# The second cross-attention of a perceiver kernel: from transposed exponentials to transposed scores

## The chip, the cores and the metric

The kernel runs on one core of one Trainium2 chip. The metric is the device time of one execution in microseconds (us): the median over several executions. Engines are named as in the profile: PE is TensorE (matrix products), PEld its weight loads, DVE VectorE, ACT ScalarE, POOL GpSimd, SP SyncE, whose queue issues the transfers (DMA). SBUF is the on-chip memory with 128 partitions, PSUM the memory of eight banks into which PE writes (a bank holds 512 fp32 values in each partition), HBM the memory of the chip. fp32r is a form of fp32 operands for PE; this kernel splits a value into a high part, rounded to that form, and a low part, the rest, and adds three products (high by high, high by low, low by high) where it wants fp32 accuracy.

## The reference

Two layers work on x of 16 batches by 64 rows by 256 features. Each reads a context `ctx_1024` of 16 x 1601 x 256. The first layer is a cross-attention with top-32, a retention step and an attention block with a mixture of experts. The second layer is the cross-attention in question, then random features, then three tree-shaped feed-forward parts. What the changed stage computes is this, with 16 heads of width 16:

```python
def _L1_xattn_ref(q, k, v, ...):            # q: layernorm(x); k = v = ctx_1024
    b, l, _ = q.shape
    ...
    qn = layernorm(q, norm_w, norm_b)
    kn = layernorm(k, norm_w, norm_b)
    vn = layernorm(v, norm_w, norm_b)
    Q = (qn @ Wq + bq).reshape(b, l, H, E)
    K = (kn @ Wk + bk).reshape(b, s, H, E)
    V = (vn @ Wv + bv).reshape(b, s, H, E)
    scale = 1.0 / jnp.sqrt(jnp.asarray(E, Q.dtype))
    scores = jnp.einsum('blhe,bshe->bhls', Q, K)
    A = jax.nn.softmax(scale * scores, axis=-1)
    O = jnp.einsum('bhls,bshd->blhd', A, V)
    O = O + Q
    out = jnp.transpose(O, (0, 2, 1, 3)).reshape(b, l, H * E)
    return layernorm(out, norm1_w, norm1_b) @ Wo + bo + out
```

Per batch there are 1601 context rows, kept as 13 chunks of 128 (the last has 65), and 16 heads x 64 queries, which makes 1024 softmax rows of 1601 scores.

## The kernel before

The program is a chain of stages. The one that changes is `phase_heads_read`, which begins with loading its parameters, normalises x and projects the queries, then goes through 16 batches, two to a turn of a loop, and ends by mixing heads and projecting the output.

**A batch.** SP loads the 1601 rows of 256 features, a context row on a partition (L1277). POOL normalises them with mean and reciprocal deviation that an earlier stage left (L1313, 13 instructions). PE transposes them into features by rows (L1386, 26 products); ACT and DVE split these into high and low (`rowsT`, L1634). Two projections follow, in units that the code calls fills: the keys, transposed, in 8 quarters of 400 to 402 columns with 6 products each (L1392), and the values, a chunk of 128 rows by 256 in 6 products (L1399), 7 fills of two chunks. ACT writes the high keys (L1518), DVE the low ones, in halves of 64 partitions (L1646), and ACT the values (L1524).

**Scores and softmax.** The 16 heads go in 8 pairs. For a pair, PE makes four quarters of scores, 128 queries (2 heads x 64) by 402 keys, two products each (L1415): the queries stand alone in their own 16 rows of a block of 128 otherwise zero, which POOL writes (`pairq`, L1328), and high and low keys stand in the two halves of the partitions. DVE takes the maximum of all 1608 columns in one instruction over four banks (L1609), ACT makes the exponentials in four instructions (L1535) into `exps` with a running sum, PE transposes `exps` chunk by chunk (L1436, 13 a pair, 104 a batch), and DVE and ACT copy the result from PSUM to `probT` (L1619, L1625, L1543). After four pairs PE weighs the values (L1454: 13 chunks x 4 products, each on a column tile of 32), and the result is divided by the sums, which are transposed for that (L1433).

**What sets the order.** The order on each engine is written out by hand: `PE_STEPS`, `ACT_STEPS` and `DVE_STEPS` give for each of the 8 pairs a string of steps (S scores of the next pair, W weigh, 0 to 3 the four groups of transposes, a to d fills of the next batch, M maximum, H and I heads and inverses), and `SLOT_FILLS` says which fills stand in which pair. The fills use banks 6 and 7 in turn, the scores banks 0 to 3, the transposes 4 and 5. After the last batch DVE adds the value bias and the queries for all rows (L1738).

## Time and profile before

| what | value |
|---|---|
| time, median of 3 executions | 1908.88 us (1906.41 to 1911.81) |
| the profiled execution: span from first to last instruction | 1909.7 us |
| PE busy over the span | 1562.7 us, 82% |
| DVE, ACT, POOL busy | 1234.9, 866.1, 370.7 us |
| `phase_heads_read`, from its first to its last instruction | 522.4 to 1641.7 us |
| of it start, 16 batches, end | 80.8, 995.6, 42.9 us |

Of the profiled execution the profile gives the span; its own time stands nowhere apart from it, and the span lies inside the three times listed. The 1909.7 us are one execution and the sums below are made against them. A busy PE says little by itself, since matrix products overlap in the pipeline and the profile models their ends: the cost of a group of products is read from the start of its first to the start of what follows on PE. An "idle before" is the gap ahead of a group and the engine's work, or the transfer, that ended it.

### The profile page before, as it was taken

To read this page: it belongs to the slowest core of one execution; us is meant where nothing else is said; L and a number is where in the kernel's file an instruction comes from. 1 tells how busy PE (TensorE), PEld (TensorE's weight loads), DVE (VectorE), ACT (ScalarE), POOL (GpSimd) and SP (SyncE) were. 2 spreads that over 40 slices of the span, in tenths; PEclk is the share of its full clock that TensorE was granted. 3 is DMA by queue.
4 is the path that set the end of the run, shared out by engine and by line. 5 is a ranking of instruction groups with operands and counts; after the bars stand their busy time and mean duration, and the time that the engine had idled before them with its cause. 6 is when DMAs were issued, how large, how long until landed. Compare 5 with 4: busy or idle time off the path is not lost. (4 is left out here: it accounts for less than half of the span.)

```text
span 1909.7 us, 32902 instructions
## 1 busy us (share of the span) xinstructions
PE 1562.7 (82%) x11828; PEld 1276.4 (67%) x11828; DVE 1234.9 (65%) x2268; ACT 866.1 (45%) x2127; POOL 370.7 (19%) x444
## 2 busy tenths in 40 slices
PE   7888876679557988988889888888898885649997
PEld 4555554469546877877778778777787773436665
DVE  4999745743554777777777767777678674554443
ACT  2444411220014666656666657566666662123322
POOL 0000000010031344224322432243224000031110
PEclk9777788679858999999999999999999997779999
DMA  9577206005030111011101110111010001020000
GB/s 331 207 278 283 90 1 254 1 1 177 10 123 1 37 37 37 1 38 37 37 2 37 37 38 1 38 37 37 2 37 1 1 1 45 14 118 38 1 1 22
DMA packets 74561, 118.97 MB, mean 62 GB/s; under 512 B 1312, under 2 KB 66976, under 8 KB 73376
## 3 DMA queue, kind: packets, MB, share of 16 engines
q1 hardware_dynamic: 74400, 116.76, 17.4%
q8 instruction: 109, 1.79, 0.4%
q14 instruction: 52, 0.43, 0.1%
HBM read 114.66 MB, written 2.10 MB: 61 GB/s over the span
## 5 line engine op out<-in xcount | busy, mean ns | idle before, releaser
L1535 ACT ACTIVATE d_exps<-psum,d_negmax 128x400 f32<-128x400 f32 (+1 forms) x512 | 297.8, 595 | 37.8 <-DVE d_negmax L1609 35.3
L1436 PE MATMUL psum<-pk,d_exps 128*128 128x128 f32 (+1 forms) x1664 | 265.8, 277 | 20.9 <-DVE d_probT L1619 11.7
L1415 PE MATMUL psum<-d_keys,d_pairq 128*128 128x402 f32 x1024 | 248.8, 376 | 20.6 <-issue 13.2
L1609 DVE TENSOR_REDUCE d_negmax<-psum 128x1 f32<-128x1608 f32 x128 | 234.4, 1831 | 48.4 <-PE psum L1415 46.9
L1646 DVE SCALAR_TENSOR_TENSOR d_keys<-psum,d_bk,d_keys 64x400 fp32r<-64x400 f32 (+1 forms) x256 | 162.4, 634 | 115.5 <-ACT d_keys L1518 108.7
L1313 POOL TENSOR_SCALAR d_rowsN<-d_rowsN,d_rowmoments 128x256 f32<-128x256 f32 x195 | 235.8, 1224 | 0.1
L1436 PEld LDWEIGHTS psum<-pk,d_exps 128*128 128x128 f32 (+1 forms) x1664 | 200.0, 141 | 47.9 <-DVE d_probT L1619 19.8
L1415 PEld LDWEIGHTS psum<-d_keys,d_pairq 128*128 128x128 f32 x1024 | 179.7, 195 | 55.6 <-ACT d_exps L1535 36.4
L1392 PE MATMUL psum<-d_rowsT,d_wk 128*128 128x400 f32 (+1 forms) x768 | 173.8, 362 | 19.6 <-DVE d_keys L1646 18.8
L1619 DVE COPY d_probT<-psum 128x512 f32<-128x512 f32 x256 | 174.0, 687 | 23.7 <-PE psum L1436 19.2
L1543 ACT ACTIVATE d_probT<-psum 128x512 f32<-128x512 f32 x128 | 76.6, 599 | 234.3 <-PE psum L1436 232.8
L1399 PE MATMUL psum<-d_wv,d_rowsT 128*128 128x256 f32 (+1 forms) x1248 | 178.0, 292 | 0.0
L1518 ACT ACTIVATE d_keys<-psum,d_bk 64x400 fp32r<-64x400 f32 (+1 forms) x256 | 151.5, 592 | 57.9 <-PE psum L1392 56.3
L1399 PEld LDWEIGHTS psum<-d_wv,d_rowsT 128*128 128x128 f32 (+1 forms) x1248 | 157.7, 189 | 0.0
L1392 PEld LDWEIGHTS psum<-d_rowsT,d_wk 128*128 128x128 f32 x768 | 133.9, 192 | 27.4 <-issue 25.9
L1386 PE MATMUL psum<-pk,d_rowsN 128*128 128x128 f32 (+1 forms) x416 | 71.3, 287 | 79.6 <-DVE d_rowsT L1634 20.3
L1323 POOL TENSOR_TENSOR d_fence<-row_mean 128x1 f32<-128x1 f32 x32 | 6.3, 196 | 669.9 <-PE psum L1415 649.0
L1386 PEld LDWEIGHTS psum<-pk,d_rowsN 128*128 128x128 f32 (+1 forms) x416 | 50.6, 145 | 93.8 <-POOL d_rowsN L1313 43.5
L1454 PE MATMUL psum<-d_probT,d_val 128*32 128x128 f32 (+1 forms) x3328 | 102.0, 278 | 5.5 <-issue 4.7
L1535 ACT ACTIVATION_READ_ACCUMULATOR d_exps<-psum,d_negmax 128x1 f32 x512 | 103.8, 203 | 0.0
L1454 PEld LDWEIGHTS psum<-d_probT,d_val 128*32 128x32 f32 (+1 forms) x3328 | 92.2, 112 | 16.2 <-issue 15.9
L2139 DVE TENSOR_SCALAR f_own<-psum,pf 128x512 f32<-128x512 f32 x48 | 36.1, 751 | 90.9 <-ACT f_ownH L2082 90.9
(376 smaller groups left out, 2472.0 us busy)
## 6 DMA issues: line engine op xcount, KB each, us to landing
a_cR<-ctx_rows_dram SPq DMA_DIRECT2D x16, 1664.0 KB, 11.6
d_rowsN<-ctx_rows_dram SPq DMA_DIRECT2D x16, 1664.0 KB, 7.8
a_cT<-ctxT_dram SPq DMA_DIRECT2D x16, 1601.0 KB, 14.2
moe_w<-moe_w_dram SPq DMA_DIRECT2D x16, 1024.0 KB, 10.1
f_raw<-trees_dram SPq DMA_DIRECT2D x3, 2048.0 KB, 9.2
pc<-pc_dram SPq DMA_DIRECT2D x1, 1968.0 KB, 11.0
pb<-pb_dram SPq DMA_DIRECT2D x1, 1666.0 KB, 6.7
pd<-pd_dram SPq DMA_DIRECT2D x1, 1164.0 KB, 5.1
```

The lines of the kernel that those rows point to most:

```text
L1313: pool.tensor_scalar(rowsN[:, u, c, :], rowsN[:, u, c, :], moments[:, u, 0, c:c + 1], moments[:, u, 1, c:c + 1], ALU.subtract, ALU.mult).t ...
L1386: last = pe.transpose(ps[:, bank, (c % 4) * P:(c % 4) * P + w], rowsN[0:w, u, c, q * P:(q + 1) * P], core.p("ident")[0:w, 0:w])
L1392: last = pe.matmul(ps[:, bank, 0:w], wk[:, a, k, j * P:(j + 1) * P], rowsT[:, c, k, s0:s0 + w], start=((k, a, c) == steps[0]), stop=((k, a ...
L1399: last = pe.matmul(ps[0:w, bank, (c % 2) * D:(c % 2 + 1) * D], rowsT[:, f, k, c * P:c * P + w], wv[:, e, k, :], start=((k, e, f) == steps[ ...
L1415: last = pe.matmul(ps[:, c, 0:SCORED], pairq[:, part, m, g, :, :], keys[:, m, g // 2, s0:s0 + SCORED], start=(part == 0), stop=(part == 1))
L1436: last = pe.transpose(ps[0:w, T_BANK + t % 2, (c % 4) * P:(c % 4 + 1) * P], exps[:, p % 2, c * P:c * P + w], core.p("ident"))
L1454: last = pe.matmul(ps[32 * g:32 * g + 32, V_BANK, m * P:(m + 1) * P], val[0:w, u, c, f:f + 32], probT[0:w, g, c, :], start=(c == 0), stop= ...
L1518: last = act.activation(keys[r, j, half, s0:s0 + w], ps[r, bank, 0:w], ACT.Identity, bias=bk[r, j:j + 1])
L1535: act.activation(exps[:, p % 2, s0:s0 + w], ps[:, c, 0:w], ACT.Exp, bias=negmax[:, p % 2:p % 2 + 1], accum_out=sums[:, p // 4, p % 4, c:c ...
L1609: dve.tensor_reduce(negmax[:, p % 2:p % 2 + 1], ps[:, 0:4, 0:SCORED], XY, ALU.max, negate=True)\
L1619: dve.tensor_copy(probT[:, g, 4 * t:4 * t + 4, :], ps[:, T_BANK + t % 2, :].rearrange("p (c n) -> p c n", c=4))\
L1646: last = dve.scalar_tensor_tensor(keys[o, m, half, s0:s0 + w], ps[r, bank, 0:w], bk[r, m:m + 1], keys[r, m, half, s0:s0 + w].bitcast(F32), ...
```

## The change

`phase_heads_read` is written anew around four ideas.

1. **Rows arrive transposed.** SP loads a copy of the context that is already features by rows (`ctxT`, L1279 of the changed kernel) in four spans (512, 384, 384, 322 columns) into `raw`. The deviations come as a row in HBM (`row_stds`, written in the stage of the attention block by two transposes, a copy and a DMA) and are broadcast to all partitions by a DMA (L1271); POOL multiplies (`scale_rows`, L1347) and makes the low parts (`low_rows`, L1354); ACT makes the high parts. The mean is taken out in the weights, once, at the start. The fills lose their transposes: 8 of keys and 7 of values are left.
2. **Keys stacked by DMA.** ACT and DVE write high and low keys on all 128 partitions to `stage`. SP then copies 32 partitions at a time (two heads) into `stack`: rows 0 to 31 high, 32 to 63 low, 64 to 95 high. These are 12 transfers of 32 x 1602 for half a batch (8 heads), with 3 small ones for the queries (high, high, low), so that one product over 96 rows gives all three terms. Rows 96 to 99 hold marks for the four key groups.
3. **A pass for maxima, then transposed scores.** For half a batch, called (b, m), which goes in 13 steps c, PE makes 16 products of 128 queries by 400 to 402 keys (`find_top`, L1457), each followed by a maximum on DVE (L1696). The negated maxima are turned (L1464) and written into the mark rows of the queries (L1711). The scores are then made again, transposed, with 128 keys as output rows and 4 x 128 queries as columns over 100 rows (`score`, L1475), so that the maximum is subtracted in the product. ACT takes the exponential of 128 x 512 straight into a ring of four buffers, from which PE weighs (`weigh`, L1491). `find_top` for the next half batch stands in steps 3 to 10 of this one.
4. **Sums by additions.** POOL adds 6 pairs of ring buffers for half a batch and DVE 5 (L1725); PE sums over partitions with a product by ones (L1503). DVE divides and adds straight to the queries with the bias in them, so L1738 goes.

The core of the diff:

```diff
             sp.dma_start(core.packs["pc"][:, :], drams["pc"]).then_inc(sig("c_params_in"), 16)
...
+            sp.wait_ge(sig("m_stds"), 1)
+            sp.dma_start(drams["row_stds"].rearrange("b (c p) -> (b c) p", p=P).rearrange("(h r) p -> r h p", h=2),
+                         stds[:, :, :]).then_inc(sig("m_stds_out"), 16)
+            sp.wait_ge(sig("m_stds_out"), 16)
...
-    PE_STEPS = ["SW012a3b", "S0a1b23", "S0a1b2c3d", "S0a1b2c3d", "SW0a1b2c3", "S0a1b2c3", "S0a1b23", "S0a1b2c3"]
...
-    DVE_STEPS = ["MH12a3b", "M1a2b3", "M1ab23cd", "IM1ab23cd", "MH1a23bc", "M1ab23c", "M1a23b", "IM1a23bc"]
...
+    CHUNKS = [(0, 4), (4, 7), (7, 10), (10, NC)]
+    SPANS = [(P * a, min(P * z, SE) - P * a) for a, z in CHUNKS]
...
+    LOWER = [("k", 0, 0), ("k", 0, 1), ("k", 0, 2), ("v", 0, 0), ("v", 1, 0), ("v", 2, 0), ("v", 3, 0), ("k", 0, 3)]
+    UPPER = [("k", 1, 0), ("k", 1, 1), ("k", 1, 2), ("v", 4, 0), ("v", 5, 0), ("v", 6, 0), ("k", 1, 3)]
...
+    FILL_AT = [{0: 0, 1: 1, 2: 2, 4: 3, 6: 4, 8: 5, 10: 6, 11: 7}, {0: 8, 1: 9, 2: 10, 4: 11, 6: 12, 8: 13, 11: 14}]
...
+    TOPS, TOP_AT = 16, 3
+    SHIFT_AT, DEN_AT, HEADS_AT = 11, 4, 6
+    POOL_ADDS = {1: 1, 3: 2, 5: 3, 7: 4, 9: 5, 11: 6}
+    VECTOR_ADDS = {4: 1, 6: 2, 8: 3, 10: 4, 12: 5}
+    S_BANK, M_BANK, V_BANK, F_BANK = 0, 2, 4, 6
...
+        raw = core.tensor(ctx, "d_raw", [P, KD, SE])
+        rowstd = core.tensor(ctx, "d_rowstd", [P, SE])
...
+        stage = core.tensor(ctx, "d_stage", [P, 2, 2, SE], F32R)
+        stack = core.tensor(ctx, "d_stack", [P, 2, 4, SE], F32R)
+        queries = core.tensor(ctx, "d_queries", [P, 2, 4, P], F32R)
...
+            def load_stack(b, m):
+                n = 2 * b + m
+                wait(sp, "d_lows", 4 * n + 4)
+                wait(sp, "d_s_ps", NC * (n - 1))
+                for part, r in ((0, 0), (0, 32), (1, 64)):
+                    sp.dma_start(queries[r:r + 32, m, :, :].bitcast(F32),
+                                 drams["queries"][part, m, :, bass.ds(b * P, P)].rearrange("(j r) n -> r j n", r=32))\
+                      .then_inc(sig(f"d_queries_in{m}"), 16)
+                for j in range(4):
+                    for part, r in ((0, 0), (1, 32), (0, 64)):
+                        sp.dma_start(stack[r:r + 32, m, j, :].bitcast(F32),
+                                     stage[32 * j:32 * j + 32, m, part, :].bitcast(F32))\
+                          .then_inc(sig(f"d_stack_in{m}{j}"), 16)
+            def batch(b, now=True, last_quarter=True, after=True, ahead=True):
+                if now:
...
+                if last_quarter:
+                    load_rows(b + 2, 3)
+                if after:
+                    load_stack(b + 1, 0)
+                if ahead:
+                    load_stds(b + 3)
+                    for q in range(3):
+                        load_rows(b + 3, q)
...
+            sp.wait_ge(sig("d_own"), 4)
+            for part, src in enumerate((ownH, ownL)):
+                sp.dma_start(drams["queries"][part].rearrange("m p n -> p m n"),
+                             src[:, 0:2 * QW].rearrange("p (m n) -> p m n", m=KD).bitcast(F32))\
+                  .then_inc(sig("d_own_out"), 16)
+            sp.wait_ge(sig("d_own_out"), 32)
+            sp.wait_ge(sig("d_marks"), 1)
+            sp.dma_start(stack[MARKS, 1, :, :].bitcast(F32), stack[MARKS, 0, :, :].bitcast(F32))\
...
+            eng.tensor_tensor(raw[:, :, s0:s0 + w], raw[:, :, s0:s0 + w],
+                              rowstd[:, s0:s0 + w].unsqueeze(1).broadcast_to([P, KD, w]), ALU.mult)\
+               .then_inc(sig(done), 1)
...
+            eng.tensor_tensor(rowsT[:, 1, :, s0:s0 + w], raw[:, :, s0:s0 + w],
+                              rowsT[:, 0, :, s0:s0 + w].bitcast(F32), ALU.subtract).then_inc(sig("d_rowlows"), 1)
...
+            pool.tensor_copy(stack[MARKS, 0, :, :],
+                             core.p("ident")[MARKS, MARKS].unsqueeze(2).broadcast_to([4, 4, SE]))\
+                .then_inc(sig("d_marks"), 1)
...
+                pool.tensor_tensor(sums[:, 0, m, :], first, ring[:, slot_of(u, m, c), :], ALU.add)\
+                    .then_inc(sig("d_sums_p"), 1)
...
+            def find_top(b, m, v):
...
+                pe.matmul(ps[:, M_BANK + v % 2, 0:w], queries[0:96, m, j, :], stack[0:96, m, j, s0:s0 + w],
+                          start=True, stop=True).then_inc(sig("d_top_ps"), 1)
...
+            def shift(b, m):
...
+                pe.matmul(ps[MARKS, M_BANK, 0:P], negmax[:, :], core.p("ident"), start=True, stop=True,
+                          tile_position=(0, 96)).then_inc(sig("d_negmax_ps"), 1)
...
+            def score(b, u, m, c):
...
+                w = P if c < NC - 1 else SL + S % 2
+                if c == 0:
+                    wait(pe, "d_shift", n + 1)
+                wait(pe, "d_exp", NC * n + c - 1)
+                for j in range(4):
+                    last = pe.matmul(ps[0:w, S_BANK + (m + c) % 2, j * P:(j + 1) * P],
+                                     stack[0:STACKED, m, j, c * P:c * P + w], queries[0:STACKED, m, j, :],
+                                     start=True, stop=True)
+                last.then_inc(sig("d_s_ps"), 1)
...
+            def weigh(b, u, m, c):
...
+                    f = m * P + 32 * g
+                    last = pe.matmul(ps[32 * g:32 * g + 32, V_BANK + m, 0:P], val[0:w, u, c, f:f + 32],
+                                     ring[0:w, slot_of(u, m, c), g * P:(g + 1) * P], start=(c == 0), stop=(c == NC - 1),
+                                     tile_position=(0, 32 * g))
+                last.then_inc(sig("d_weigh_ps"), 1)
...
+                        last = pe.matmul(ps[32 * g:32 * g + 32, V_BANK + m, P:2 * P], ones[:, 0:32],
+                                         sums[:, e, m, g * P:(g + 1) * P], start=(e == 0), stop=(e == 1),
+                                         tile_position=(0, 32 * g))
...
+                    nxt = (b, 1) if m == 0 else (b + 1, 0)
+                    ahead = fills or m == 0
+                    for c in range(NC):
+                        score(b, u, m, c)
+                        if fills and c in FILL_AT[m]:
+                            fill(b + 1, 1 - u, FILL_AT[m][c])
+                        if ahead and TOP_AT <= c < TOP_AT + TOPS // 2:
+                            for v in range(2):
+                                find_top(*nxt, 2 * (c - TOP_AT) + v)
+                        if ahead and c == SHIFT_AT:
+                            shift(*nxt)
+                        if c >= 2:
+                            weigh(b, u, m, c - 2)
+                        elif m or not first:
+                            weigh(*before(b, u, m), NC - 2 + c)
+                        if c == DEN_AT and (m or not first):
+                            denominators(*before(b, u, m)[::2])
...
+            for v in range(TOPS):
+                find_top(0, 0, v)
+            shift(0, 0)
...
+                act.activation(rowsT[:, 0, :, s0:s0 + w], raw[:, :, s0:s0 + w], ACT.Copy).then_inc(sig("d_rows"), 1)
...
+                    act.activation(stage[:, j, 0, s0:s0 + w], ps[:, bank, 0:w], ACT.Identity, bias=bk[:, j:j + 1])\
                        .then_inc(sig("d_fill"), 1)
...
+                act.activation(ring[0:w, slot_of(u, m, c), :], ps[0:w, S_BANK + (m + c) % 2, :], ACT.Exp)\
...
+            def take_low(b, u, n):
...
+                    dve.scalar_tensor_tensor(stage[:, m, 1, s0:s0 + w], ps[:, bank, 0:w], bk[:, m:m + 1],
+                                             stage[:, m, 0, s0:s0 + w].bitcast(F32), ALU.add, ALU.subtract)\
+                       .then_inc(sig("d_lows"), 1)
...
+            def take_top(b, m, v):
...
+                dve.tensor_reduce(top[:, m, v:v + 1], ps[:, M_BANK + v % 2, 0:min(w, S - s0)], X, ALU.max)\
+                   .then_inc(sig("d_top"), 1)
...
+                dve.tensor_reduce(negmax[:, :], top[:, m, :].rearrange("p (j q) -> p j q", j=4), X, ALU.max, negate=True)\
                    .then_inc(sig("d_negmax"), 1)
...
+                dve.tensor_copy(queries[MARKS, m, :, :], ps[MARKS, M_BANK, 0:P].unsqueeze(1).broadcast_to([4, 4, P]))\
+                   .then_inc(sig("d_shift"), 1)
...
+                dve.tensor_tensor(sums[0:w, 1, m, :], first, ring[0:w, slot_of(u, m, c), :], ALU.add)\
+                   .then_inc(sig("d_sums_d"), 1)
...
+                dve.reciprocal(invT[:, :], ps[:, V_BANK + m, P:2 * P]).then_inc(sig("d_inv"), 1)
...
+                dve.tensor_tensor(on[:, :], ps[:, V_BANK + m, 0:P], invT[:, :], ALU.mult).then_inc(sig("d_on"), 1)
...
+                dve.scalar_tensor_tensor(QT[:, m, cols], on[:, 0:L], core.p("parity")[:, 0:1], QT[:, m, cols],
+                                         ALU.mult, ALU.add).then_inc(sig("d_even"), 1)
+                wait(dve, "d_even", n + 1)
+                dve.scalar_tensor_tensor(QT[:, m, cols], on[:, L:2 * L], core.p("parity")[:, 1:2], QT[:, m, cols],
+                                         ALU.mult, ALU.add).then_inc(sig("d_heads"), 1)
...
-                dve.scalar_tensor_tensor(OT[:, m, :], OT[:, m, :], bv[:, m:m + 1], QT[:, m, :], ALU.add, ALU.add)\
```

In the middle of a batch PE has this order before (scores of a pair, its transposed exponentials, fills of the next batch):

```order
L1415 MATMUL psum<-d_keys,d_pairq 128x402 x8
L1436 MATMUL psum<-pk,d_exps 128x128 x4
L1392 MATMUL psum<-d_rowsT,d_wk 128x402 x6
L1436 MATMUL psum<-pk,d_exps 128x128 x4
L1399 MATMUL psum<-d_wv,d_rowsT 128x256 x12
L1436 MATMUL psum<-pk,d_exps 128x128 x4
L1392 MATMUL psum<-d_rowsT,d_wk 128x400 x6
```

and at steps 4 and 5 of a half batch this one now (scores, a fill, maxima of the next half batch, weighing, denominators of the one before):

```order
L1475 MATMUL psum<-d_queries,d_stack 128x128 x4
L1442 MATMUL psum<-d_wv,d_rowsT 128x256 x12
L1457 MATMUL psum<-d_stack,d_queries 128x400 x2
L1491 MATMUL psum<-d_ring,d_val 32x128 x4
L1503 MATMUL psum<-d_ring,d_ones 32x128 x8
L1475 MATMUL psum<-d_queries,d_stack 128x128 x4
L1457 MATMUL psum<-d_stack,d_queries 128x402
L1457 MATMUL psum<-d_stack,d_queries 128x400
L1491 MATMUL psum<-d_ring,d_val 32x128 x4
```

The transposes are gone, the weighing has moved from one block of 104 records into every step, and the products for maxima stand between the scores of one step and the next. DVE before has, for a pair and a half, one long maximum, three copies and the low keys in halves:

```order
L1609 TENSOR_REDUCE d_negmax<-psum 128x1
L1619 COPY d_probT<-psum 128x512 x2
L1625 COPY d_probT<-psum 65x128
L1646 SCALAR_TENSOR_TENSOR d_keys<-psum,d_bk,d_keys 64x400 x2
L1609 TENSOR_REDUCE d_negmax<-psum 128x1
L1619 COPY d_probT<-psum 128x512 x2
```

and at the end of a half batch now:

```order
L1725 TENSOR_TENSOR d_ring<-d_ring 128x512
L1696 TENSOR_REDUCE d_top<-psum 128x1 x4
L1725 TENSOR_TENSOR d_ring<-d_ring 128x512
L1696 TENSOR_REDUCE d_top<-psum 128x1 x4
L1704 TENSOR_REDUCE d_negmax<-d_top 128x4
L1725 TENSOR_TENSOR d_ring<-d_ring 128x512
L1687 SCALAR_TENSOR_TENSOR d_stage<-psum,d_bk,d_stage 128x322
L1711 CAST d_queries<-psum 4x512
```

The copies out of PSUM are gone; short maxima and additions of ring buffers have taken their place, and the write of the shifts (L1711) now stands behind a low part of the next batch's keys (L1687). SP, which before issues one load of rows for a batch,

```order
L1277 ISA
L1277 DMA d_rowsN<-ctx_rows_dram 128x13x256
L1285 ISA
L1277 ISA
L1277 DMA d_rowsN<-ctx_rows_dram 128x13x256
```

now issues for a batch, in this order:

```order
L1289 DMA d_queries<-queries_dram 32x4x128 x3
L1294 DMA d_stack<-d_stage 32x1602 x12
L1279 DMA d_raw<-ctxT_dram 128x2x321
L1289 DMA d_queries<-queries_dram 32x4x128 x3
L1294 DMA d_stack<-d_stage 32x1602 x12
L1271 DMA d_rowstd<-row_stds_dram 128x1602
L1279 DMA d_raw<-ctxT_dram 128x2x512
L1279 DMA d_raw<-ctxT_dram 128x2x384 x2
```

Thirty-six transfers stand where one stood, and the raw rows of a later batch stand behind the copies to `stack` on the same queue.

## Rows read from the trace of the kernel before

**Rows 1.** Windows of the stage: PE, PEld, DVE, ACT, POOL busy (count); PEclk; DMA; GB/s.

```profile
522.40:603.20 80.80, 48.04 (x186) 38.99 (x187) 40.08 (x110) 19.74 (x38) 24.12 (x31) 0.62 0.24 79
603.20:1598.80 995.60, 868.86 (x8376) 775.55 (x8375) 717.32 (x1185) 628.51 (x1618) 302.35 (x384) 0.99 0.08 24
1598.80:1641.70 42.90, 19.23 (x80) 15.84 (x80) 21.55 (x51) 5.42 (x8) 0.00 (x0) 0.64 0.18 49
```

**Rows 2.** Timeline, PE alone, one batch: start, duration, line, operation, count, idle before.

```profile
1135.58 0.48 PE L1433 MATMUL psum<-pk,pd 128*128 128x128 f32 x2
...
1142.61 1.35 PE L1392 MATMUL psum<-d_rowsT,d_wk 128*128 128x402 f32 x6
1143.79 0.60 PE L1436 MATMUL psum<-pk,d_exps 128*128 128x128 f32 x4
1144.15 1.66 PE L1399 MATMUL psum<-d_wv,d_rowsT 128*128 128x256 f32 x12
1145.65 0.60 PE L1436 MATMUL psum<-pk,d_exps 128*128 128x128 f32 x4
...
1147.85 1.74 PE L1415 MATMUL psum<-d_keys,d_pairq 128*128 128x402 f32 x8
1149.42 0.60 PE L1436 MATMUL psum<-pk,d_exps 128*128 128x128 f32 x4
...
1169.06 1.72 PE L1415 MATMUL psum<-d_keys,d_pairq 128*128 128x402 f32 x8
1170.71 3.05 PE L1454 MATMUL psum<-d_probT,d_val 128*32 128x128 f32 x104
1173.69 1.09 PE L1436 MATMUL psum<-pk,d_exps 128*128 128x128 f32 x8
...
1198.06 0.46 PE L1433 MATMUL psum<-pk,pd 128*128 128x128 f32 x2
```

**Rows 3.** Waits of PE from 690 to 1490 us: total, times, longest.

```profile
PE psum L1386 <- DVE d_rowsT L1634: 19.7, 11, 1.8
PE psum L1386 <- POOL d_rowsN L1313: 18.3, 13, 2.2
PE psum L1386 <- DVE d_keys L1646: 16.7, 12, 1.4
```

**Rows 4.** Groups by form, whole span: busy us, mean ns, idle before.

```profile
L1313 POOL TENSOR_SCALAR d_rowsN<-d_rowsN,d_rowmoments 128x256 f32<-128x256 f32 x195 | 235.8, 1224 | 0.1
L1609 DVE TENSOR_REDUCE d_negmax<-psum 128x1 f32<-128x1608 f32 x128 | 234.4, 1831 | 48.4 <-PE psum L1415 46.9
...
L1646 DVE SCALAR_TENSOR_TENSOR d_keys<-psum,d_bk,d_keys 64x400 fp32r<-64x400 f32 x192 | 121.7, 634 | 104.9 <-ACT d_keys L1518 101.4
...
L1524 ACT ACTIVATE d_val<-psum 128x512 f32<-128x512 f32 x96 | 58.3, 607 | 22.3 <-PE psum L1399 22.3
...
L1328 POOL TENSOR_TENSOR d_pairq<-d_tileqL,pd 128x256 fp32r<-128x256 f32 x64 | 38.1, 617 | 0.0
...
L1929 POOL TENSOR_TENSOR f_wL<-f_raw,f_wH 128x1024 fp32r<-128x1024 f32 x12 | 31.2, 2608 | 253.7 <-ACT f_wH L2055 253.7
L1016 PE MATMUL psum<-c_disp,moe_w 128*128 128x128 f32 x256 | 29.7, 275 | 0.0
```

**Rows 5.** Windows: SBUF to HBM from sixteen partitions; HBM to all partitions.

```profile
1609.50:1614.50 5.00, 0.00 (x0) 0.00 (x0) 0.00 (x0) 0.09 (x1) 0.00 (x0) 0.63 0.78 188
522.40:534.00 11.60, 3.57 (x16) 3.48 (x16) 7.10 (x29) 0.21 (x1) 0.00 (x0) 0.50 0.96 319
```

**Rows 6.** Timeline of the stage's start: queries projected, first exponential.

```profile
565.04 9.45 PE L216 MATMUL psum<-d_probT,pd 128*128 128x512 f32 x16 [0.95 <-ACT d_probT L187]
...
600.44 0.60 ACT L1535 ACTIVATE d_exps<-psum,d_negmax 128x400 f32<-128x400 f32 x1
```

**Rows 7.** Timeline after the last batch.

```profile
1599.04 2.48 DVE L1738 SCALAR_TENSOR_TENSOR d_OT<-d_OT,d_bv,d_QT 128x1024 f32<-128x1024 f32 x2
```

More of the change, by code:

```diff
@@ L1263, in batches @@
                 one(i, 1)
-            one(B // 2 - 1, 0)
-            last()
+            one(B // 2 - 1, 0, rows=False)
+            one(B // 2 - 1, 1, rows=False, fills=False)
         def wait(eng, name, value):
@@ L1333, in _ @@
[L1333 to L1345 removed]
+            pool.memset(ones[:, :], 1.0).then_inc(sig("d_ones"), 1)
@@ new lines, in batch @@
+            def batch(i, u, rows=True, fills=True):
+                b = 2 * i + u
+                for m in range(2):
+                    for c in range(NC):
+                        if c in POOL_ADDS:
+                            add(b, u, m, c)
+                        if rows and m == 0 and c in SCALE_AT:
+                            scale_rows(pool, b + 2, SCALE_AT[c], "d_scaled")
+                        if rows and m == 1 and c in ROWS_AT:
+                            low_rows(pool, b + 2, ROWS_AT[c])
@@ L1347, in _ @@
+            batches(pool, batch)
         @block.tensor
@@ L1575, in _ @@
+            act.wait_ge(sig("d_own"), 4)
+            for m in range(KD):
+                act.activation(QT[:, m, :], QT[:, m, :], ACT.Identity, bias=bv[:, m:m + 1]).then_inc(sig("d_QT_bv"), 1)
+            batches(act, batch)
             for f in range(0, HD1 // 2, 2):
```

736 lines of the change are left out of this document (329 added, 407 removed).

## The prediction

> **What bounds the kernel now.** I read the windows first. The stage has 80.8 us of start, 995.6 us for sixteen batches and 42.9 us of end [rows 1]; nearly all that changes lies in the 995.6. There PE's records cover 868.9 us, DVE's 717.3, ACT's 628.5, POOL's 302.4, and the DMA share is 0.08. PE leads, at a granted clock of 0.99 of its 2.4 GHz level. The timeline of PE gives one batch: the pair of L1433 products comes back after 1198.06 - 1135.58 = 62.5 us [rows 2]. From start to start: a key fill 1.18 us (1142.61 to 1143.79), a value fill 1.50, the eight scores of a pair 1.57 (1147.85 to 1149.42), four transposes 0.36, the 104 weighing records 2.98 [rows 2].
>
> PE's own work in a batch is then 8 x 1.18 = 9.4 for keys, 6.5 x 1.50 = 9.8 for values, 8 x 1.57 = 12.6 for scores, 8 x (3 x 0.36 + 0.11) = 9.5 for transposed exponentials, 26 x 0.11 = 2.9 for transposed rows, 2 x 2.98 = 6.0 for weighing, 0.4 for inverses: 50.6. The other 11.9 us of the period are waits. The list of PE's waits puts 54.7 us, over 800 us or 12.8 batches, at the row transposes alone: for the split on DVE, for POOL's normalised rows, for low keys [rows 3]. That is 4.3 a batch; the rest is spread thin.
>
> **What goes.** Scores, both kinds of transposes, weighing and inverses: 12.6 + 9.5 + 2.9 + 6.0 + 0.4 = 31.4 us of PE. The fills keep their product count and columns, 19.2 us.
>
> **What comes on PE.** The maxima take 32 products of 400 columns, half as many as the scores before: 32 x 1.57/8 = 6.3. The second scores take 104 products of 128 columns. No row shows an fp32r product this narrow. A transpose of 128 columns takes 0.36/4 = 0.09 to (1.09 - 0.60)/4 = 0.12 [rows 2]; a plain fp32 product of 128 columns at L1016 is two records, 29.7 us over 128 calls, 0.232 each [rows 4]. I take 0.11, since the 400-column products here run as single passes (0.196 for 400 columns, 0.49 ns a column, so that 128 columns would be 0.06 plus a floor): 11.4. Weighing keeps its 208 records, 6.0, but stands in 26 groups instead of 2. Entering the column tiles cost 1.65 - 1.57 = 0.08 at 1169.06 [rows 2]; leaving and refilling a short group isn't shown. I charge 0.2 for each group, near the 2.98/13 = 0.23 of one chunk: 5.2; bounds 0 and 0.55 (two full latencies of 0.275, the mean of a 128-column record at L1016 [rows 4]). Denominators are 32 narrow records, 32 x 2.98/104 = 0.9, with two changes 1.3. The shift adds 0.5. Sum: 6.3 + 11.4 + 11.2 + 1.3 + 0.5 = 30.7, almost what went. PE's work alone thus stays: 49.9 against 50.6. **The gain must come from the 11.9 us of waits.**
>
> The Trainium skill, "TensorEngine Tiling (Array Packing)", section "Key Properties", says that a change of tiling mode drains TensorE. The 0.08 on entering speaks against a full drain each time; by a full drain the weighing is rival C2 below.
>
> **Which waits are left.** Row transposes go, with their 4.3 us. Score groups no longer stand behind a 1.83 us maximum and four exponentials. New ones come in two places. First, PE makes two `find_top` products a step into two banks and DVE must take each: a maximum of 400 costs between 1831/4 = 458 and the 634 ns of a 400-column form [rows 4]; I take 0.57. A DVE addition of 128 x 512 I put at 0.69, from the same 634 ns of a two-input operation. Such a step holds DVE 2 x 0.57 + 0.69 = 1.83, PE 1.26 when it has no fill; some of it is made up in steps with fills: 1.6 us a half batch. Second, the shift: PE's product, the write at L1711 behind a low part of keys at L1687, then the next half batch's first score: 1.1. Together 2 x 2.7 = 5.4 a batch, bounds 2 and 11.9.
>
> **New period: 49.9 + 5.4 = 55.3 us**, against 62.5.
>
> **The cover.** DVE in a batch: 32 maxima 18.2, eight low parts 5, ten additions 6.9, heads and small ones 3.3: 33 us. ACT: 26 exponentials at 0.61 (the 128x512 row has 607 ns [rows 4]), 9 of fills, 3.5 of rows: 29. POOL: SBUF operations of two inputs take 617/256 = 2.4 and 2608/1024 = 2.5 ns an element of a partition [rows 4]; scaling and low parts are 6408 elements, 15.4 us, and 12 additions of 512 are 14.7: 30 us. Queued behind each addition on POOL are the scaled rows of a batch two later, which have a whole batch of slack. All are under 55.3.
>
> DMA is the new thing. It moved 24 GB/s here [rows 1]; now a half batch copies 12 x 205 KB and 3 x 64 KB = 2.66 MB. No row shows SBUF to SBUF. From sixteen partitions to HBM the trace moved 188 GB/s, from HBM to all partitions 319 [rows 5]. I take 188, the nearer, since these transfers too touch few partitions: 14.1 us, plus 2.4 for fixed parts, per half batch of 27.7. They begin when the half batch begins, the first of four pieces is wanted at step 3 (some 6 us in) and the last at step 9; 7 us of steps follow the last. 2.4 + 14.1 + 7 = 23.5, which fits. Behind them on SP's queue stand 2.46 MB of raw rows and deviations a batch, 8 us at 319. At nothing to hide behind the copies would cost 33 us a batch.
>
> The Trainium skill, "SBUF — State Buffer", section "Who interferes with whom", says that a DVE instruction with two SBUF inputs and a GpSimd instruction that reads SBUF exclude each other. No run here shows it: the large DVE operations of this stage take one input from PSUM. By it the ten additions would lengthen something by 0.7 us a batch, 11 us in all, and the sum would be 1808.
>
> **The sum.** First batch 55.3 + 5; fourteen more at 55.3, 774; the last, with no fills and half the maxima, 45 (its PE work alone is 49.9 - 19.2 - 3.2 = 27.5, and chains through ACT, POOL and DVE fill some of the rest). That makes 880, against 995.6: -116. Start: the queries, projected from 565.04 on [rows 6], now go through HBM and back, and the first stack must land before the first maxima; the first exponential stood at 600.44 [rows 6]. I add 5; bounds 0 and 15, the upper if the copy of the marks (6408 elements at 2.4 ns, 15 us on POOL) comes late. End: the two L1738 operations, 2.48 us [rows 7], go. Writing the deviations adds 0.5. 1909.7 - 116 + 5 - 2.5 + 0.5 = **1797 us**. The profiled span of 1909.7 stands 0.8 above the median of 1908.88; that doesn't matter here.
>
> **Rivals.** *A, the forecast:* 1797. *B, slow copies.* If SBUF to SBUF moves 130 GB/s, a half batch needs 2.4 + 20.5 + 7 = 29.9 us, the period is 59.8, and the time 1797 + 15 x 4.5 = 1865. The period of before, 31.2 a half, is reached at 122 GB/s. For it: 32 partitions at either end; against: the 188 of a similar narrow transfer. *C, slower than before: a 128-column fp32r product costs what a plain fp32 one does*, 0.232 for 0.11. That adds 104 x 0.122 = 12.7 a batch, less 2.5 that the waits for maxima absorb: 10.2 x 16 = 163, so 1960. It decides from 0.20 us a product. For it: no narrow fp32r product in the trace, and both kinds read four-byte operands; against: the 400-column ones show one record a call. *C2, each change to and from column tiles drains PE:* 0.55 instead of 0.2 for 26 groups, 9.1 a batch, so 1943. *D, POOL at the 1224/256 = 4.8 ns an element of L1313 [rows 4]:* 60.3 us a batch; ACT waits for the addition of four steps earlier before it writes a ring buffer, so POOL sets the period: 1797 + 16 x 5 = 1877. *E, the change doesn't free the waits:* PE's work is the same, and two-bank hand-offs with DVE (maxima), ACT (exponentials, fills) and POOL (ring buffers) keep 11 us of waits: a period of 61 to 62.5, 1885 to 1909.
>
> **Chances.** A 0.57, B 0.12, C 0.10, C2 0.04, D 0.06, E 0.11. About 0.3% either way, 1903 to 1915, is what a measurement of this kernel can tell from no change. Faster: A, B, D and most of E, 0.82; same: the end of E, 0.04; slower: C and C2, 0.14. A's own range is 1725 (no cost for tile changes, few waits) to 1845. The range 1730 to 1905 leaves out C, C2 and a sliver at each side.
>
> **What would show it.** In the changed kernel's windows a batch of 55 us with PE's gaps near 5. The timeline of PE: from one group of L1475 to what follows about 0.45 for four products (C: 0.9). Start of L1491 to what follows 0.43 (C2: near 0.8). The waits of PE: L1457 for L1696 and L1475 for L1711 on top; if L1457 waits for `d_stack` transfers it is B, if L1475 or the exponentials wait for POOL's additions it is D. Copies to `stack` from issue to landing 15 to 20 us a half batch. The prediction is wrong if the period is over 60 with PE's products at the prices above, or if several of these waits chain within a step.

## The result, and the profile after

The changed kernel takes 1939.35 us (median of 4 executions, 1937.26 to 1954.26) against 1907.64 for the kernel before in the same comparison; the ratio is 1.018, with a 95% interval of 1.014 to 1.022. It is slower by 32 us, where 1797 was forecast. The profiled execution has a span of 1935.5 us.

The page opens with the busy times; the second part shows the clock in 40 slices.

```profile
PE 1627.7 (84%) x11422; PEld 1191.9 (62%) x11422; DVE 1081.9 (56%) x2033; ACT 665.9 (34%) x1210; POOL 524.9 (27%) x349
...
PEclk8877788679777899888888988898879875779999
```

DVE, ACT and the instruction counts have gone down, as forecast. In the slices of this stage, though, the clock stands at 8 and 9 where PEclk of before has rows of nines. The windows of the sixteen batches, as in [rows 1], say it in one number: the column before the DMA share.

```profile
610.00:1630.00 1020.00, 934.40 (x7959) 694.49 (x7958) 564.27 (x967) 420.34 (x698) 451.52 (x304) 0.85 0.47 113
```

The granted clock is 0.85 where it was 0.99. Since it has two levels here, 1 and 0.5, a mean of 0.85 is 0.15/0.5 = 0.30 of the time at the 1.2 GHz level, 306 us. PE's records cover 934.4 of the 1020 us, and 0.30 of that is 280 us. If PE is the bound there, work that runs 280 us at half clock would take 140 at full clock; so 140 us, 8.8 a batch, is an estimate of what the clock can have cost. The time lies 142 us above the forecast.

The waits of PE over the same stretch (total, times, longest), against [rows 3]:

```profile
PE psum L1457 <- DVE d_top L1696: 59.3, 30, 2.3
PE psum L1475 <- issue: 10.2, 5, 2.4
PE psum L1475 <- DVE d_queries L1711: 8.9, 13, 0.7
PE psum L1457 <- DMA d_stack<-d_stage: 3.7, 1, 3.7
```

The waits have fallen. PE's idle time was (995.6 - 868.9)/16 = 7.9 us a batch [rows 1]; the whole list, of which four lines stand above, now makes 84.5/16 = 5.3, with 5.4 forecast. (The 11.9 us of the prediction are more than 7.9, since they hold all that its start-to-start prices left over.) But the waits lie in few pieces: 30 pauses at L1457, nearly all of 1.9 to 2.3 us, one at each half batch. The timeline of PE shows one, and what comes behind it (start, duration, idle before, as in [rows 2]):

```profile
1103.00 0.66 PE L1475 MATMUL psum<-d_queries,d_stack 100*128 100x128 f32 x4
1103.49 0.62 PE L1457 MATMUL psum<-d_stack,d_queries 96*128 96x402 f32 x2
1104.05 0.43 PE L1491 MATMUL psum<-d_ring,d_val 128*32 128x128 f32 x8
1104.41 0.66 PE L1475 MATMUL psum<-d_queries,d_stack 100*128 100x128 f32 x4
1104.91 0.87 PE L1442 MATMUL psum<-d_wv,d_rowsT 128*66 128x256 f32 x6
1108.07 0.93 PE L1457 MATMUL psum<-d_stack,d_queries 96*128 96x400 f32 x2 [2.29 <-DVE d_top L1696]
...
1113.29 1.12 PE L1475 MATMUL psum<-d_queries,d_stack 100*128 100x128 f32 x4
1114.20 1.92 PE L1434 MATMUL psum<-d_rowsT,d_wk 128*128 128x322 f32 x6
```

Up to 1104.91 a step costs what was forecast: scores 0.49 (0.44 forecast), maxima 0.56 or 0.46 (0.39), weighing 0.36 (0.43). At 1108.07 PE comes back from a pause of 2.29 us; some 2 us later the same groups are nearly twice as long: four score products 1.12 against 0.66, a key fill of 322 columns 1.92. The windows of the slow stretch and of a later one give 0.56 and 1.00:

```profile
1109.50:1117.00 7.50, 7.50 (x49) 5.24 (x48) 3.96 (x9) 2.32 (x4) 2.54 (x2) 0.56 0.00 0
1124.00:1139.00 15.00, 15.00 (x153) 11.81 (x154) 8.04 (x15) 6.96 (x12) 10.31 (x7) 1.00 0.59 133
```

PE has no idle time at all in either; only its clock differs. Between 610 and 1400 us there are 23 such pauses, and 22 have a stretch at the lower level behind them, mostly of 3 to 17 us; the one that has none is the shortest, 1.73 us.

What DVE and POOL do in such a pause, in the next batch:

```profile
1168.20 0.95 DVE L1734 RECIPROCAL pd<-psum 128x128 f32<-128x128 f32 x1
...
1169.18 0.29 DVE L1736 TENSOR_TENSOR pd<-psum,pd 128x128 f32<-128x128 f32 x1
...
1169.63 0.74 DVE L1738 SCALAR_TENSOR_TENSOR d_QT<-pd,d_QT 128x64 f32 x1 [0.16 <-DVE pd L1736]
...
1170.24 1.27 POOL L1386 TENSOR_TENSOR d_ring<-d_ring 128x512 f32<-128x512 f32 x1
...
1170.41 1.18 DVE L1741 SCALAR_TENSOR_TENSOR d_QT<-pd,d_QT 128x64 f32 x1
...
1171.51 0.68 DVE L1725 TENSOR_TENSOR d_ring<-d_ring 128x512 f32<-128x512 f32 x1
```

This is `take_heads`, four operations one behind the other from 1168.20 to 1171.59, and an addition, all ahead of the maxima of steps 7 and 8 in DVE's order. PE can't make another maxima product until a bank is taken. L1741 works on 64 columns and takes 1.18 us; it ends, at 1171.59, just after POOL's addition has ended (1171.51).

The last batch is a case of its own. It has no fills, and it begins with the wait of 3.7 us for the copies to `stack`. Behind that the clock stays at the lower level to the end of the batch, though PE's records cover nearly all of the time:

```profile
1580.00:1625.00 45.00, 44.15 (x339) 29.85 (x332) 19.82 (x35) 13.12 (x22) 12.76 (x10) 0.50 0.15 33
```

The theory from here on: DVE's chain at step 6 makes PE pause once a half batch, and behind such a pause the clock is at its lower level for some microseconds; the time is lost there, not in the pause. The rivals: the transfers, which went from 24 to 113 GB/s, or the new mix of products take the clock; or the pauses themselves are the cost.

### The profile page after: what moved, and what is told of

The parts are those of the page before. It is cut to its first block and busy times, and to the rows that moved or that the text cites. A ratio compares the mean times of both kernels' runs of the same rounds, so it can differ in the third digit from the quotient of the medians.

```text
span 1935.5 us, 32050 instructions
## 1 busy us (share of the span) xinstructions
PE 1627.7 (84%) x11422; PEld 1191.9 (62%) x11422; DVE 1081.9 (56%) x2033; ACT 665.9 (34%) x1210; POOL 524.9 (27%) x349
## 5 line engine op out<-in xcount | busy, mean ns | idle before, releaser
L1603 ACT ACTIVATE d_ring<-psum 128x512 f32<-128x512 f32 (+1 forms) x416 | 248.4, 597 | 440.1 <-PE psum L1475 426.7
L1696 DVE TENSOR_REDUCE d_top<-psum 128x1 f32<-128x400 f32 (+2 forms) x512 | 270.2, 569 | 205.7 <-PE psum L1457 201.9
L1386 POOL TENSOR_TENSOR d_ring<-d_ring 128x512 f32<-128x512 f32 x192 | 245.1, 1276 | 492.4 <-ACT d_ring L1603 492.4
L1475 PE MATMUL psum<-d_queries,d_stack 100*128 100x128 f32 (+1 forms) x1664 | 312.5, 318 | 20.6 <-issue 10.2
L1475 PEld LDWEIGHTS psum<-d_queries,d_stack 100*128 100x128 f32 (+1 forms) x1664 | 249.9, 217 | 124.0 <-issue 91.5
L1457 PE MATMUL psum<-d_stack,d_queries 96*128 96x400 f32 (+1 forms) x512 | 177.5, 425 | 69.7 <-DVE d_top L1696 60.8
L1687 DVE SCALAR_TENSOR_TENSOR d_stage<-psum,d_bk,d_stage 128x384 fp32r<-128x384 f32 (+2 forms) x128 | 81.3, 635 | 238.8 <-ACT d_stage L1583 238.8
L1491 PE MATMUL psum<-d_ring,d_val 128*32 128x128 f32 (+1 forms) x3328 | 210.1, 320 | 0.0
L1434 PE MATMUL psum<-d_rowsT,d_wk 128*128 128x384 f32 (+2 forms) x768 | 199.3, 403 | 3.0 <-POOL d_rowsT L1355 2.5
L1355 POOL TENSOR_TENSOR d_rowsT<-d_raw,d_rowsT 128x1024 fp32r<-128x1024 f32 (+1 forms) x64 | 129.0, 2018 | 119.7 <-ACT d_rowsT L1574 119.7
L1457 PEld LDWEIGHTS psum<-d_stack,d_queries 96*128 96x128 f32 x512 | 95.2, 217 | 90.0 <-DVE d_top L1696 78.1
L1491 PEld LDWEIGHTS psum<-d_ring,d_val 128*32 128x32 f32 (+1 forms) x3328 | 78.4, 117 | 104.2 <-issue 78.2
L1725 DVE TENSOR_TENSOR d_ring<-d_ring 128x512 f32<-128x512 f32 (+1 forms) x160 | 111.5, 697 | 25.7 <-ACT d_ring L1603 24.6
L1347 POOL TENSOR_TENSOR d_raw<-d_raw,d_rowstd 128x768 f32<-128x768 f32 (+2 forms) x60 | 105.3, 1758 | 2.9 <-DMA d_raw<-ctxT_dram 2.9
```

Of the source, the lines that this page charges most:

```text
L1347: eng.tensor_tensor(raw[:, :, s0:s0 + w], raw[:, :, s0:s0 + w], rowstd[:, s0:s0 + w].unsqueeze(1).broadcast_to([P, KD, w]), ALU.mult)\
L1355: eng.tensor_tensor(rowsT[:, 1, :, s0:s0 + w], raw[:, :, s0:s0 + w], rowsT[:, 0, :, s0:s0 + w].bitcast(F32), ALU.subtract).then_inc(sig("d ...
L1386: pool.tensor_tensor(sums[:, 0, m, :], first, ring[:, slot_of(u, m, c), :], ALU.add)\
L1434: last = pe.matmul(ps[:, bank, 0:w], wk[:, a, k, j * P:(j + 1) * P], rowsT[:, c, k, s0:s0 + w], start=((k, a, c) == steps[0]), stop=((k, a ...
L1457: pe.matmul(ps[:, M_BANK + v % 2, 0:w], queries[0:96, m, j, :], stack[0:96, m, j, s0:s0 + w], start=True, stop=True).then_inc(sig("d_top_p ...
L1475: last = pe.matmul(ps[0:w, S_BANK + (m + c) % 2, j * P:(j + 1) * P], stack[0:STACKED, m, j, c * P:c * P + w], queries[0:STACKED, m, j, :], ...
```

## The experiments

**1. Filling the pause with useless work.** At step 8, ahead of the maxima, 18 products go into the score bank that the next step overwrites.

```diff
+                        if ahead and c == 8:
+                            wait(pe, "d_exp", NC * (2 * b + m) + c)
+                            for _ in range(WARM):
+                                pe.matmul(ps[:, S_BANK + (m + c + 1) % 2, 0:P], stack[0:STACKED, m, 0, 0:P],
+                                          queries[0:STACKED, m, 0, :], start=True, stop=True)
```

> The changed kernel with useless work added: at step 8 of each half batch, where PE waits about 2 us for DVE's maxima, 18 extra products of 100x128x128 go into the score bank that the next step overwrites (about 2 us of PE; 31 of them in the run). Theory 1 (the time is lost to the granted clock, which falls a few us after each such pause): the pause is filled, the clock of the batches rises from 0.85 to over 0.95 and the kernel gets faster than 1939 although it does more, 1820 to 1870. Theory 2 (the pauses themselves, or the transfers to the stack, cost the time, and the clock falls for another reason): the clock stays at 0.85 and the time at 1935 to 1960.

1903.7 us, 35 us faster than the changed kernel with 31 x 2 us of products added. No loss of time from the pauses alone could give that. But the clock is 0.92 over 610 to 1400 us (0.87 in the changed kernel) and not over 0.95; it still fell behind the filled place at 7 of some 25 half batches in that stretch, and behind gaps at the loop's turn, which the list calls issue. Neither theory had its number: right in direction, half in size.

```profile
PE psum L1476 <- DVE d_queries L1717: 12.0, 17, 0.7
PE psum L1476 <- issue: 10.5, 5, 2.9
PE psum L1458 <- DVE d_top L1702: 4.3, 12, 0.4
```

**2. The same with wide products.** Eight of 512 columns in place of the 18 of 128.

> As the run with 18 extra products of 128 columns at step 8, but with 8 extra products of 512 columns in their place, again about 2 us of PE. Theory 1a (the clock follows how much PE streams, and narrow products with their weight loads leave it half idle, which is why 18 of them held the clock in only about half of the places): the clock of the batches rises from 0.91 to 0.96 or more and the time falls from 1904 to 1830 to 1870. Theory 1b (only an idle PE matters, and what was left in that run came from the gaps at the loop's turn): the clock stays near 0.91 and the time near 1900.

1873.9 us (ratio to the kernel before 0.985, 0.981 to 0.988), clock 0.95 over 610 to 1400 us. One fall was left behind step 8 (at 1388 us, after a rest of the pause of 0.46); the others stand at the gaps of the loop's turn. With the same occupation of PE in time, about 2 us, wide products let the clock fall in 1 place and narrow ones in 7 (so the narrow ones had held it in some 18 of 25 places, not in half as the expectation has it). The time came out 4 us over the expected range and the clock just under it.

**3. The heads at another step.** One number changes.

```diff
-    SHIFT_AT, DEN_AT, HEADS_AT = 11, 4, 6
+    SHIFT_AT, DEN_AT, HEADS_AT = 11, 4, 12
```

> The changed kernel with one number changed: DVE takes the heads (L1734 to L1741) at step 12 of a half batch, behind the shift, instead of step 6 between maxima. Theory 1: the 1.9 to 2.3 us pauses of L1457 for L1696 go, with them the falls of the clock; clock of the batches over 0.95, time 1770 to 1820. Theory 2 (the clock falls for another reason, as the transfers): the pauses go, 59 us in all, clock stays 0.85, time 1870 to 1890. Theory 3 (the chain is only moved, to the first fills of the next half batch): a wait of like length at L1434 for L1687, time 1920 to 1940.

1789.8 us; ratio to the kernel before 0.939 (0.934 to 0.943). 150 us go, where the pauses were 59 us. The window of its batches up to the last one, the same with the last one, and the last one alone:

```profile
610.00:1421.00 811.00, 779.98 (x7557) 593.36 (x7555) 499.76 (x922) 403.52 (x670) 440.61 (x292) 0.98 0.57 139
610.00:1472.00 862.00, 828.81 (x7926) 626.59 (x7928) 521.26 (x962) 418.77 (x695) 455.82 (x304) 0.95 0.55 134
1421.00:1472.00 51.00, 48.83 (x374) 33.23 (x374) 21.50 (x40) 15.26 (x26) 15.22 (x12) 0.51 0.24 51
```

The 0.98 is to be held against 0.87 in the changed kernel (610 to 1575 us) and the 0.95 against its 0.85. The last batch stays at the lower level here too, and so it does in all other versions of the new kernel (0.50 over 1400 to 1447 us in experiment 8, over 1380 to 1428 in experiment 10). PE's waits from 610 to 1400 us:

```profile
PE psum L1475 <- DVE d_queries L1711: 17.3, 24, 0.7
PE psum L1475 <- issue: 13.0, 5, 2.8
```

L1457 no longer waits for L1696. The chain of the heads has become shorter as well: L1741 takes 285 ns, since at step 12 no operation of POOL runs beside it. Two half batches take 1054.74 - 1000.34 = 54.4 us (between the L1503 groups), where the changed kernel takes 1131.74 - 1067.08 = 64.7:

```profile
1000.34 0.62 PE L1503 MATMUL psum<-d_ring,d_ones 128*32 128x128 f32 x16
...
1054.74 0.62 PE L1503 MATMUL psum<-d_ring,d_ones 128*32 128x128 f32 x16
```

```profile
1067.08 0.62 PE L1503 MATMUL psum<-d_ring,d_ones 128*32 128x128 f32 x16
...
1131.74 0.62 PE L1503 MATMUL psum<-d_ring,d_ones 128*32 128x128 f32 x16
```

**4. The pause put back.** In the kernel of experiment 3, a DVE reduction that nothing needs stands at step 6.

```diff
+                        if c == 6:
+                            dve.tensor_reduce(pause[:, :], core.p("ident").unsqueeze(1).broadcast_to([P, 24, P]), X,
+                                              ALU.max)
```

> The kernel with the heads at step 12, with a DVE reduction of 3072 elements, about 3.2 us, that nothing needs, at step 6 where the heads stood. Theory 1: the pauses of about 2 us at L1457 and the falls of the clock come back, clock of the batches 0.85 to 0.90, time 1900 to 1945. Theory 4 (it was the heads' own operations or their meeting with POOL, not the time they hold DVE): time under 1830.

1990.4 us, 200 us slower than without it, for 32 reductions that took 3.34 us each, 107 us of DVE. The clock is 0.81 over 610 to 1400 us. A pause and what follows it:

```profile
1064.21 0.66 PE L1476 MATMUL psum<-d_queries,d_stack 100*128 100x128 f32 x4
1064.71 0.87 PE L1443 MATMUL psum<-d_wv,d_rowsT 128*66 128x256 f32 x6
1067.82 1.18 PE L1458 MATMUL psum<-d_stack,d_queries 96*128 96x400 f32 x2 [2.24 <-DVE d_top L1697]
1068.93 0.66 PE L1492 MATMUL psum<-d_ring,d_val 128*32 128x128 f32 x8
1069.52 1.12 PE L1476 MATMUL psum<-d_queries,d_stack 100*128 100x128 f32 x4
```

The pauses and the slow stretches come back, with a DVE operation that has nothing to do with the heads: what matters isn't what the heads compute, but that DVE is held in front of the maxima. The time came out beyond the range of theory 1, 51 us above the changed kernel, and the waits don't say why: 30 pauses at L1457 with 59.4 us in all and 2.2 at most, against 59.3 and 2.3. What differs is the clock, 0.81 for 0.87. Why the same pauses cost more clock here is open.

**5. The transfers.** The copies to `stack` are cut to 64 of 1602 columns from the second batch on, so that scores are made of old keys.

```diff
+                cut = SE if b <= 0 else 64
...
-                        sp.dma_start(stack[r:r + 32, m, j, :].bitcast(F32),
-                                     stage[32 * j:32 * j + 32, m, part, :].bitcast(F32))\
+                        sp.dma_start(stack[r:r + 32, m, j, 0:cut].bitcast(F32),
+                                     stage[32 * j:32 * j + 32, m, part, 0:cut].bitcast(F32))\
```

> The changed kernel with the copies from stage to stack cut to 64 columns of 1602 from the second batch on (the scores of later batches are then made of old keys); the number of transfers is the same. Theory 1: clock and pauses unchanged, 1930 to 1945. Theory 2 (the traffic on SBUF takes the clock or the time): clock over 0.95, time under 1880.

1938.9 us in one execution. Between 610 and 1400 us the traffic falls from 123 to 50 GB/s and the clock is 0.85 (0.87 with the copies). The traffic takes neither time nor clock.

**6. The same in the kernel before.** A DVE reduction of 1024 elements lengthens a pause that is there already.

```diff
+                if n == 4:
+                    dve.tensor_reduce(pause[:, :], core.p("ident").unsqueeze(1).broadcast_to([P, 8, P]), X, ALU.max)
                 dve.tensor_tensor(rowsT[:, 1, k, cols]
```

> The kernel before with one DVE reduction of 1024 elements, some 1.1 us, put ahead of the split of a group of transposed rows (L1634) in every batch, where PE already waits 1.8 us. Theory 1 (a pause of over some 2 us costs clock behind it): clock of the batches falls well below 0.99 and the time rises by more than 16 x 1.1 = 18 us, 1945 to 1990. Theory 2 (the clock is not a matter of pauses of this size): clock 0.99, time 1915 to 1928.

1944.7 us, ratio 1.020 (1.018 to 1.022): 38 us for 16 reductions that took 1.21 us each, 19 us of work, just short of the expected range. The clock is 0.96 over 610 to 1630 us, where the kernel before has 0.97 (first line; its 0.99 [rows 1] is of the batches alone):

```profile
610.00:1630.00 1020.00, 874.00 (x8390) 779.43 (x8388) 725.42 (x1213) 629.75 (x1615) 302.35 (x384) 0.97 0.08 25
610.00:1630.00 1020.00, 879.31 (x8229) 784.40 (x8227) 728.47 (x1191) 626.04 (x1604) 301.85 (x384) 0.96 0.07 23
```

Over 610 to 1400 us it is 0.97 for 0.99, and there 1-us windows add up to 51 us at the lower level, where the kernel before has 17. Pauses of 1.8 us in this place [rows 2, 3] had been nearly free of it; pauses of 2.9 and 3.3 us aren't. So it isn't the new kernel's products alone that make the clock fall.

**7. POOL's additions.** They are cut to 4 of 512 columns, so the sums over keys are incomplete.

```diff
-                pool.tensor_tensor(sums[:, 0, m, :], first, ring[:, slot_of(u, m, c), :], ALU.add)\
+                pool.tensor_tensor(sums[:, 0, m, 0:4], first[:, 0:4], ring[:, slot_of(u, m, c), 0:4], ALU.add)\
```

1871.6 us in one execution. L1741 in the changed kernel, and here (groups by form: busy us, mean ns, idle before):

```profile
L1741 DVE SCALAR_TENSOR_TENSOR d_QT<-pd,d_QT 128x64 f32 x24 | 30.6, 1277 | 0.8
```

```profile
L1741 DVE SCALAR_TENSOR_TENSOR d_QT<-pd,d_QT 128x64 f32 x24 | 6.8, 285 | 0.8
```

1277 ns was 285 ns of work and 992 ns of waiting for POOL: in one half batch L1741 ends 0.08 us after POOL's addition, in the next 0.08 us after its scaling of rows (L1347), with 1.18 and 1.37 us. PE's pauses shrink from at most 2.3 to at most 1.4 us, and 68 us go, some 40 of them by the clock: it is 0.91 for 0.87 over 610 to 1400 us, over a stage of 1000 us (0.04/0.5) x 1000 = 80 us less at half clock. L1738 did not get shorter, 836 ns before and 995 now: it now meets POOL's low part of rows (L1355) in one half batch and the scaling in the next, which are both still there, and again ends 0.08 us after them.

**8. PE's loop written out.** In the kernel of experiment 3, the PE program goes through all batches without a loop.

```diff
+            if unrolled:
+                for i in range(1, B // 2 - 1):
+                    one(i, 0)
+                    one(i, 1)
...
-            batches(pe, batch)
+            batches(pe, batch, unrolled=True)
```

> The kernel with the heads at step 12, and PE's loop over pairs of batches written out. The run with the heads late has five gaps of 2.4 to 2.8 us on PE that end in issue, one at each turn of the loop, and 27 of its 47 us of low clock stand behind two of them and 17 behind a third. If the loop's turn is the cause: the gaps go, 13 us, and with them most of those 47 us at half clock, worth some 19; time 1790 to 1755 to 1770. If it is something else that meets at that place (DVE's shift): gaps stay, 1785 to 1795.

1755.4 us, ratio to the kernel before 0.920 (0.918 to 0.923). The five gaps are gone, and the clock is 1.00 over 610 to 1400 us:

```profile
610.00:1400.00 790.00, 768.98 (x7590) 585.76 (x7588) 500.65 (x926) 407.05 (x674) 443.04 (x294) 1.00 0.59 144
```

```profile
PE psum L1480 <- DVE d_queries L1716: 19.9, 30, 0.7
```

**9. The same loop in the kernel before.**

```diff
-            batches(pe, batch, lambda: batch(B // 2 - 1, 1, fills=False))
+            batches(pe, batch, lambda: batch(B // 2 - 1, 1, fills=False), unrolled=True)
```

> The kernel before with PE's loop over pairs of batches written out and nothing else. It has five gaps of 2.3 to 2.6 us at the loop's turn, ending in issue, and smaller ones at the same place of L1454 and L1386. If the loop's turn alone costs: 13 us of gaps and 3 to 7 of clock go, 1906 to 1885 to 1892. If the gaps of before overlap waits that come anyway: 1900 to 1908. Either way less than the 35 us that the same edit gave the kernel with the heads late, where low clock stood behind the gaps.

1891.5 us, ratio 0.992 (0.990 to 0.994), 15 us. The loop's turn costs there too, with the clock at 0.99 over 610 to 1400 us in both kernels, but less than half of what it costs in the new kernel (34 us). The gain doesn't belong to the change; 1755.4 is to be held against 1891.5 for what the new algorithm brings: 7%.

**10. The shift first.** In the kernel of experiment 8, DVE writes the shifts (L1711) ahead of the low part of keys at step 11.

```diff
+                        if ahead and c == SHIFT_AT:
+                            take_shift(*nxt)
                         if fills and c in FILL_AT[m]:
                             take_low(b + 1, 1 - u, FILL_AT[m][c])
...
-                        if ahead and c == SHIFT_AT:
-                            take_shift(*nxt)
```

> The kernel with the heads at step 12 and PE's loop written out, with DVE's write of the shifts (L1711) ahead of the low part of the keys (L1687) at step 11. There L1475 waits 0.66 us at each half batch for L1711, 30 times. If that wait comes from the low part ahead of it in DVE's order: it goes, 1755 to 1730 to 1742. If it is the length of the chain itself (maxima, product, write): under 5 us, 1750 to 1756.

1741.6 us; ratio to the kernel before 0.914 (0.911 to 0.916). The 20 us of waits for the shift are gone, 14 us in the time. What is left on PE between 610 and 1400 us is one kind:

```profile
PE psum L1462 <- DMA d_stack<-d_stage: 5.5, 6, 3.5
```

PE's records cover 784 of these 790 us, and a batch takes 51 us. This is the fastest version tried.

## Why the prediction was wrong

**The step that failed is the first one: "at a granted clock of 0.99 of its 2.4 GHz level".** That row was taken over to the new kernel as if it were a property of the stage. It was an outcome of the old order of pauses and products. The forecast then asked for each wait only how long it is, and added them. The sum of the waits came out (5.3 us a batch for 5.4), by luck, as the next paragraph shows; but the price of a wait also has what the clock does behind it, and that was some 8.8 us a batch, more than the whole gain of 7.2. From the first exponential to the last operation on the heads 1020.0 us pass (607.96 to 1627.95), where 880 were forecast: 963.5 for the first fifteen batches, where 834 were forecast, and 56.5 for the last, where 45 were. The prediction named this sign itself: a period over 60 us (it is 64.7) with PE's products at the forecast prices. None of the rivals has the clock; the two that ended slower, C and C2, were dearer products and lay outside the range, so 1730 to 1905 had no case at 1939.

**The wait was put in the wrong place.** "Some of it is made up in steps with fills: 1.6 us a half batch" saw waits of 0.57 in many steps. In the trace these hardly exist. What there is instead is DVE's chain for the heads, which the cover paragraph put among "heads and small ones 3.3" a batch, as busy time hidden beside other work. It takes 3.4 us in the half batch shown, in one piece (0.95, 0.29, 0.74, 1.18 and gaps), so nearly 7 a batch for 3.3, and right between maxima that PE needs two banks of. The shift, forecast at 1.1 us a half batch, makes PE wait 8.9 us in all 32. The order rows of DVE showed the places where maxima and additions meet; the step with `HEADS_AT` wasn't followed in time.

**Two SBUF inputs beside POOL.** The prediction gave the rule of the Trainium skill ("SBUF — State Buffer", section "Who interferes with whom") a price of 0.7 us a batch, for the additions, and said that nothing showed it. Experiment 7 shows it: 992 of the 1277 ns of L1741 are waiting for POOL. DVE's additions, for which I had priced it, hardly suffer (699 ns, 684 with POOL's small), and the small operations in the chain do, where each microsecond is one of PE's pause.

**What held.** A step of PE at full clock costs 1.31 to 1.41 us where 1.26 was forecast; 128-column products in fp32r cost 0.12 each, so rival C falls; changes to and from column tiles cost no more than was charged: four weighing calls with both changes take 0.36, so C2 falls. The copies move faster than the 188 GB/s assumed (a window of 1126 to 1131 us, mostly of copies, has 222 at a DMA share of 0.97) and experiment 5 takes them out of the matter: B falls. POOL's additions take 1276 ns for 512 columns, 2.5 ns an element: D falls. The start came 7.5 us later (first exponential at 607.96, [rows 6]) for 5 forecast. The end, from the last operation on the heads to the last addition, was shorter by 3.5 (1599.00 to 1641.39, then 1627.95 to 1666.85) for 2.5. With the pauses gone the batch took 54.4 us for 55.3 forecast, and the kernel 1789.8 for 1797. That this is so close is partly luck: of the 5.4 us of waits a batch only (862 - 829)/16 = 2.1 are there, mostly for the loop's turn and the shift, and a clock of 0.95 over 829 us of PE costs about as much as the rest, 0.05/0.5 x 829/2 = 41 us or 2.6 a batch, more than half of it in the last batch.

**What stays open.** Why the clock falls behind 7 of the filled pauses in experiment 1 and 1 in experiment 2 isn't settled beyond the width of the products. Nor do the runs give a length of pause from which the clock falls. In the kernel before five gaps of 2.3 to 2.6 us at the loop's turn have one slow stretch behind them; in experiment 3 five of 2.4 to 2.8 have three; in experiment 7, 12 of 13 pauses of 1.4 us have one; and in experiment 4 the same pauses as in the changed kernel cost more. Why the last batch runs at the lower level without a pause inside it is open too; half of the 45 us, 22, is an estimate of what it costs, and no version of the new kernel is without it. The gap at the loop's turn is 1.5 to 2.9 us on PE in every kernel that has it; that this is instruction fetch wasn't tried. The Trainium skill, "Runtime: NRT & Kernel Launch", section "Instruction fetch mechanics", says that a taken branch to a target outside the fetched pages stalls the engine; experiments 8 and 9 agree with that, and with other costs of a branch.

## What to carry to other kernels

A granted clock read from an old profile is a result of the old order, not a constant. Before it goes into a sum, list the single pauses of PE in the new order with their lengths, above all where a chain of small operations on another engine stands between hand-offs of few buffers, and ask for the time with some of the work behind each of them at the lower level. A chain that is "only" some per cent of an engine's busy time belongs at a step where nobody waits for that engine. And when a kernel with fewer waits isn't faster, look at the clock column before looking for more work.
